# One decoder layer on one core: two query tiles share one burst of value products, the second half's norm chain works by columns, and its turning comes three slots later

## The reference, cut to what matters

```
x = x + attention(layernorm(x))            # 32 heads of 32, 8 key/value heads, RoPE, causal
x = x + fake_quant(layernorm(x)) @ fake_quant(ctx)   # ctx: 2 x 1024 x 1024
x = x + layernorm(x) @ W_org.T + mixture_of_low_rank(layernorm(x))

attention: qkv = h @ w_qkv.T + b_qkv ; q, k = rope(q), rope(k)
           softmax(mask(q k^T / sqrt(32))) v ; then @ w_o.T + b_o
layernorm: (x - mean) / sqrt(var + 1e-5)
```

## Time and profile before

| | |
|---|---|
| median of three executions | 717.89 us (717.77 to 718.95) |
| profiled execution: own time, span | 717.73 us, 715.9 us |
| TensorE busy, share | 660.2 us, 92% |
| VectorE busy | 430.2 us, 60% |
| ScalarE busy | 424.7 us, 59% |
| GpSimd busy | 281.2 us, 39% |
| mean granted TensorE clock | 0.976 |

### The profile page before, as it was taken

The page is one execution under the profiler, slowest core; times in us unless marked ns, Lnnn a source line. Parts: engine busy times, 40 slices in busy tenths (PEclk is TensorE's granted clock), DMA queues, the critical chain, the costliest instruction groups (busy, mean ns, idle before and its releaser), DMA issues.

```text
span 715.9 us, 12713 instructions
## 1 busy us (share of the span) xinstructions
PE 660.2 (92%) x4512; PEld 530.3 (74%) x4512; DVE 430.2 (60%) x1137; ACT 424.7 (59%) x1025; POOL 281.2 (39%) x301
## 2 busy tenths in 40 slices
PE   4996899999999899999989699999999698999998
PEld 3985677898777678777756577777878576788886
DVE  6796677875877634677676966442326788811122
ACT  5425678878787747599977675755315782611320
POOL 2046645534444354455320720506715024814520
PEclk9998999999999999999999899999999989999999
DMA  7646854752555733225561340505326352614102
GB/s 264 227 152 187 244 164 124 213 149 76 144 159 160 201 87 99 94 56 150 178 181 60 100 130 1 147 1 156 124 75 234 100 187 82 189 47 117 44 16 102
DMA packets 43934, 93.46 MB, mean 131 GB/s; under 512 B 5505, under 2 KB 5889, under 8 KB 42433
## 3 DMA queue, kind: packets, MB, share of 16 engines
q1 hardware_dynamic: 34416, 66.45, 29.3%
q0 software_dynamic: 3696, 15.73, 9.5%
q10 hardware_dynamic: 5760, 10.49, 4.0%
HBM read 72.72 MB, written 19.92 MB: 129 GB/s over the span
## 4 chain that ended last, share of the span: by engine, by line
PE 72%; DVE 12%; ACT 6%; issue 4%; POOL 4%; DMA 1%; ACTq 0%; DVEq 0%
PE dense L1040 47%; PE probt L932 8%; PE score L920 5%; PE pv L947 5%; POOL w_lo L1653 2%; DVE stats L1333 2%; ACT prob_all L1131 2%; DVE xres L1435 2%; PE score L1040 1%; DVE w_lo L1269 1%; PE misc L956 1%; PE probt L901 1%; ACT w_hi L1084 1%; PE misc L986 1%; PE misc L901 1%
## 5 line engine op out<-in xcount | busy, mean ns | idle before, releaser
L1040 PE MATMUL dense<-w_hi,act_t 128*128 128x512 f32 (+1 forms) x684 | 226.0, 391 | 5.4 <-POOL act_t L1664 1.8
L1289 DVE CUSTOM_DVE_ANT_0 prob_all<-score,mask_sb 128x128 f32<-128x128 f32 (+3 forms) x256 | 123.2, 488 | 121.0 <-PE score L920 119.1
L1653 POOL TENSOR_TENSOR w_lo<-stage,w_hi 128x512 fp32r<-128x512 f32 x85 | 110.1, 1303 | 201.8 <-ACT w_hi L1084 201.6
L1131 ACT ACTIVATE prob_all<-prob_all,neg_max 128x128 f32<-128x128 f32 (+3 forms) x256 | 142.7, 558 | 37.4 <-DVE neg_max L1289 36.0
L1040 PEld LDWEIGHTS dense<-w_hi,act_t 128*128 128x128 f32 x684 | 128.5, 193 | 28.4 <-issue 3.8
L1040 PE MATMUL dense<-act_t,w_hi 128*128 128x512 f32 x408 | 138.2, 420 | 3.3 <-DVE xres L1435 2.1
L1040 PE MATMUL dense<-w_lo,act_t 128*128 128x512 f32 (+1 forms) x372 | 135.5, 385 | 1.6 <-ACT w_lo L1089 1.4
L932 PE MATMUL probt<-ident_sb,prob_all 128*128 128x128 f32 x640 | 113.7, 277 | 5.1 <-ACT prob_all L1140 4.5
L1084 ACT ACTIVATE w_hi<-stage 128x512 fp32r<-128x512 f32 x117 | 72.0, 623 | 45.6 <-PE dense L1040 34.8
L1140 ACT ACTIVATE prob_all<-probt 128x128 f32<-128x128 f32 (+3 forms) x160 | 68.5, 428 | 47.8 <-PE probt L932 47.0
L932 PEld LDWEIGHTS probt<-ident_sb,prob_all 128*128 128x128 f32 x640 | 80.0, 142 | 22.0 <-issue 7.5
(11 more groups left out here) (168 smaller groups left out, 858.7 us busy)
## 6 DMA issues: line engine op xcount, KB each, us to landing
q_stack<-rope_dram POOLq DMA_DIRECT2D x15, 768.0 KB, 7.3
stage<-in_w_qk SPq DMA_DIRECT2D x40, 256.0 KB, 3.0
rope_dram<-act_t ACTq DMA_DIRECT2D x40, 256.0 KB, 2.5
stage<-in_w_o SPq DMA_DIRECT2D x32, 256.0 KB, 2.9
stage<-in_ctx_kv SPq DMA_DIRECT2D x24, 256.0 KB, 3.4
stage<-in_w_org SPq DMA_DIRECT2D x24, 256.0 KB, 3.1
xres<-in_x SPq DMA_DIRECT2D x8, 512.0 KB, 7.0
prob_all<-in_x SPq DMA_DIRECT2D x8, 512.0 KB, 5.9
```

The lines of the kernel that those rows point to most:

```text
L1040: last = engine.matmul(dst, lhs, rhs, start=(k == 0 and c == 0), stop=(k == g.kts - 1 and c == len(pairs) - 1))
L1131: engine.activation(prob[:, u % P_SLOTS, 0:length], prob[:, u % P_SLOTS, 0:length], ACT.Exp, bias=neg_max[:, m:m + 1], scale=-1.0, accum_o ...
L1289: engine.tensor_tensor_reduce(prob[:, u % P_SLOTS, 0:length], score_bank[u % 2][:, 0:length], mask_sb[:, S - length:S], -1.0, HIGHEST, ALU ...
L1653: engine.tensor_tensor(slot_lo(p, 0, NW), raw_of(p), slot_hi(p, 0, NW).bitcast(F32), ALU.subtract).then_inc(g_piece, 1)
```

## The change

The four edits are:

1. `values` takes a list of tiles. Tiles 0 and 1 of a group are multiplied in one burst, where tile 1 stood (slot `s + 12`); tiles 2 and 3 keep theirs. `t_pv` now counts three per group. The turned probabilities of tile 0 (128 columns) and tile 1 (256 columns) of a head share one slot of `prob_t`: tile 0 in columns 0 to 127, tile 1 behind it.
2. The first two operations of `norm_chain_of_all` are issued for each of the four columns by itself: eight operations for two.
3. The second sequence's turning, and the taking out with it, are three slots later: slots 28, 30, ... 42. The last two lie in slots 40 and 42, which hold units 0 and 2.
4. `constants` moves from slot 10 to slot 5 (`HEAD - 3`).

```diff
+BURSTS = (0, 1), (2,), (3,)
...
-                at = HEAD + 17 + 4 * t + 2 * half
+                at = HEAD + 20 + 4 * t + 2 * half
                 self.note("turn", at, (1, 1, t, half))
                 self.note("tokens", at, (1, 1, t, half))
...
+        def place(u):
+            gi, i, h = unit(u)
+            return GROUP * (len(BURSTS) * gi + max(i - 1, 0)) + h
+        def turned_to(u, a, b):
+            start = P if unit(u)[1] == 1 else 0
+            return prob_t[:, place(u) % PROBT_SLOTS, start + a:start + b]
...
-            def values(w):
-                gi, i = divmod(w, NT)
+            def values(gi, tiles):
                 b, g = divmod(gi, NKV)
-                u = w * GROUP
-                for h in range(GROUP):
-                    e.wait_ge(*probt_done(u + h))
-                e.wait_ge(*evacuated("v", b, 0, i))
-                if i == 0 and gi:
+                for i in tiles:
+                    for h in range(GROUP):
+                        e.wait_ge(*probt_done((gi * NT + i) * GROUP + h))
+                if 0 in tiles and gi:
                     e.wait_ge(v_attn, gi)
-                for c in range(i + 1):
-                    for h in range(GROUP):
-                        last = engine.matmul(
-                            pv_bank[h * HD:(h + 1) * HD, i * P:(i + 1) * P], values_sb[:, b, c, g * HD:(g + 1) * HD],
-                            prob_t[:, (u + h) % PROBT_SLOTS, c * P:(c + 1) * P], start=(c == 0), stop=(c == i))
+                for i in tiles:
+                    e.wait_ge(*evacuated("v", b, 0, i))
+                    for c in range(i + 1):
+                        for h in range(GROUP):
+                            last = engine.matmul(
+                                pv_bank[h * HD:(h + 1) * HD, i * P:(i + 1) * P], values_sb[:, b, c, g * HD:(g + 1) * HD],
+                                turned_to((gi * NT + i) * GROUP + h, c * P, (c + 1) * P), start=(c == 0), stop=(c == i))
                 last.then_inc(t_pv, 1)
...
-                if 0 <= u - PV_LAG < UNITS and (u - PV_LAG) % GROUP == GROUP - 1:
-                    values((u - PV_LAG) // GROUP)
+                if 0 <= u - PV_LAG < UNITS:
+                    gi, i, h = unit(u - PV_LAG)
+                    for tiles in BURSTS:
+                        if (i, h) == (tiles[-1], GROUP - 1):
+                            values(gi, tiles)
...  (both take_out_turned, ScalarE and VectorE)
-                if u >= PROBT_SLOTS:
-                    e.wait_ge(t_pv, (u - PROBT_SLOTS) // GROUP + 1)
+                if place(u) >= PROBT_SLOTS:
+                    e.wait_ge(t_pv, (place(u) - PROBT_SLOTS) // GROUP + 1)
...  (norm_chain_of_all)
-                ln(engine.tensor_scalar(w, var, EPS, -ROOT_SCALE, ALU.add, ALU.mult))
+                for t in range(NT):
+                    ln(engine.tensor_scalar(w[:, t:t + 1], var[:, t:t + 1], EPS, -ROOT_SCALE, ALU.add, ALU.mult))
                 wait_ln()
-                ln(engine.tensor_scalar(ln_i[:, :], w.bitcast(I32), -0.5, RSQRT_SEED, ALU.mult, ALU.add))
+                for t in range(NT):
+                    ln(engine.tensor_scalar(ln_i[:, t:t + 1], w[:, t:t + 1].bitcast(I32), -0.5, RSQRT_SEED, ALU.mult, ALU.add))
...  (VectorE's loop)
                 if j == HEAD + 2:
                     e.wait_ge(t_keys, 1)
                     engine.tensor_copy(keys_d[:, :, :].rearrange("p k e -> p (k e)"), misc_bank[:, 0:KD * E]).then_inc(v_keys, 1)
+                if j == HEAD - 3:
                     constants()
```

More of the change, by code:

```diff
@@ L754, in fetch @@
                 elif plan.stage_slot[p] >= STAGE_SLOTS:
-                    e.wait_ge(t_pv, GROUPS * NT)
+                    e.wait_ge(t_pv, GROUPS * len(BURSTS))
                 engine.dma_start(raw_of(p), source_of(p)).then_inc(d_stage[plan.stage_slot[p]], 16)
@@ L1137, in take_out_turned @@
                 e.wait_ge(t_turned, u + 1)
-                if u >= PROBT_SLOTS:
-                    e.wait_ge(t_pv, (u - PROBT_SLOTS) // GROUP + 1)
-                engine.activation(prob_t[:, u % PROBT_SLOTS, 0:length], probt_bank[u % 2][:, 0:length],
+                if place(u) >= PROBT_SLOTS:
+                    e.wait_ge(t_pv, (place(u) - PROBT_SLOTS) // GROUP + 1)
+                engine.activation(turned_to(u, 0, length), probt_bank[u % 2][:, 0:length],
                                   ACT.Copy).then_inc(a_probt, 1)
@@ L1295, in take_out_turned @@
                 e.wait_ge(t_turned, u + 1)
-                if u >= PROBT_SLOTS:
-                    e.wait_ge(t_pv, (u - PROBT_SLOTS) // GROUP + 1)
-                engine.tensor_copy(prob_t[:, u % PROBT_SLOTS, 0:length],
+                if place(u) >= PROBT_SLOTS:
+                    e.wait_ge(t_pv, (place(u) - PROBT_SLOTS) // GROUP + 1)
+                engine.tensor_copy(turned_to(u, 0, length),
                                    probt_bank[u % 2][:, 0:length]).then_inc(v_probt, 1)
@@ L1308, in scale_values @@
                 e.wait_ge(a_inv, gi + 1)
-                e.wait_ge(t_pv, NT * gi + NT)
+                e.wait_ge(t_pv, len(BURSTS) * (gi + 1))
                 engine.tensor_tensor(attn, pv_bank[:, :], attn, ALU.mult).then_inc(v_attn, 1)
@@ L1427, in rotate @@
                     if m >= ROPES - LATE_ROPES:
-                        e.wait_ge(t_pv, NKV * NT)
+                        e.wait_ge(t_pv, NKV * len(BURSTS))
                         e.wait_ge(g_add, m)
```

## The result

The changed kernel took 714.23 us as the median of 14 executions (713.21 to 717.62); the kernel before, run beside it 14 times on the same chip, took 718.19 us (716.67 to 720.65). The ratio is 0.9946, 95% interval 0.9934 to 0.9957: 3.9 us faster, with 3.1 and 4.7 as ends. The profiled execution took 713.21 us with a span of 711.4 us, against 717.73 and 715.9 before; the mean granted clock was 0.978 against 0.976. TensorE was busy 655.1 us (660.2 before).

A forecast was written before the change was run, and what follows sets the result against it. Bound by TensorE's own sequence in attention and, from 47 to 86 us, a VectorE-ScalarE-GpSimd chain. 3.3 + 1.2 + 0.5 = 5.0 us off 717.73 gives 712.7, with 0.16 for the median 712.9 us; 8-in-10 range 709.2 to 716.4.

The forecast's parts named there:

- The burst: Attention: 16 fewer bursts at 0.24 us take 3.9 us off TensorE's queue; 3.3 us of gain counted.
- 85% taken: Attention: share of the 3.9 us saved on TensorE assumed to reach the time, 3.3 us; bounds 0 and 3.9.
- second rival, "hidden anyway": Slot s + 8: another engine is late in most groups, TensorE's saving becomes waits for maxima; 717.1 us, chance 0.12.
- The wait for `v_attn`: Tile 0's value products waited 1.6 us for `scale_values`; in slot s + 12 that goes, 1.2 us gained.
- the slower rival: Slot s + 12: the burst of 24 records delays the next score 0.22 us, starving ScalarE and VectorE; 720.9 us, chance 0.06.
- The constants: Head, slot 5: unheld by GpSimd there, the rotation that frees the dense bank ends 1.8 us earlier; bounds 0 and 2.35.
- The columns: Norm chain: one-column operations aren't held by GpSimd, the hold moves to two products; 0.2 us gained, bounds 0.0 and 1.6.
- The arrival at slot 40: Head: ScalarE reaches slot 40 1.9 us earlier, at 76.5 instead of 78.4 us.
- the head: Constants, columns and later turning together: unit 4 turned 0.3 to 0.6 us earlier, 0.5 taken; bounds -1.5 and +3.
- the zigzag: Slots 40 and 42: half tiles pass through ScalarE then VectorE, about 1.4 us each, 2.8 us lost.
- The addition of job 5: GpSimd, before unit 4: needs all three rotations of job 5; to start at 83.2 us against 83.51.
- the first rival, "the head pays too": Products don't meet GpSimd, job 5's addition comes 2 us earlier or more, plus the burst's whole 3.9; 710.3 us, chance 0.29.

The follow-up runs named there:

- The second series: The unmodified changed kernel run once more beside the kernel before, in a later series: 716.00 us against 718.52, ratio 0.9963.
- the burst alone: Kernel before with only tiles 0 and 1 sharing a burst; constants, chain and turning as before: 717.43 us, ratio 0.9987.
- the kernel that has no shared burst: Kernel before with early constants, chain by columns and later turning, value products as before: 714.81 us, ratio 0.9956.
- the turning back: Changed kernel with the second sequence's turning three slots earlier again, where it was before: 713.79 us, ratio 0.9937, six executions.
- the scaling later: Changed kernel with `scale_values` three slots later in all groups but the last of each sequence: 712.64 us, ratio 0.9936.
- the split burst: Changed kernel with tile 0's products in their own burst again, ahead of the score in slot s + 12: 719.41 us, ratio 1.0018.
- the wide chain: Changed kernel with the norm chain's first two operations on all four columns again, run in two series: 716.39 us, 0.9973; 715.02 us, 0.9962.

## Why the prediction came out as it did, step by step

The sum, 712.9 us, was 1.3 us from the measured 714.2, and 5.0 us of gain stood against 3.9 measured. That is luck in good part, since its two terms were wrong in opposite directions. The second series, with 2.7 us, lies further off.

**The burst: too large by 1.6 to 3.5 us.** Predicted 3.3 + 1.2 = 4.5; by time 1.0 (with -0.7 and 2.5 as ends); by the marks from group 0 to 15, 1.6 us in the changed kernel's second run, 1.8 with the burst alone and 2.9 in the first, with 0.4 of the same drift in the kernel that has no shared burst. The working of the *cost* erred low: 0.33 us and not 0.24, since the turning behind the score is late as well by 0.11 us. Groups 2, 7, 9, 10 and 15 show the sum, with the burst gone and with it put back. The failed step is the next one: "The six waits for a maximum over 256 units say that it is seldom eaten", and 85% taken. A count of waits in a queue that is as slow as its partners says nothing about how near the partners are: VectorE was late by less than the burst that TensorE did at that place, so it didn't show. With the burst alone, waits for the maximum rose from 3.2 to 6.0 us, of which 1.6 us had been the wait for `v_attn`. Moving `scale_values` three slots on made groups 1 to 7 another 1.7 us shorter. The prediction's second rival, "hidden anyway", is right for groups 1, 3, 4, 6 and 8 (in 8 it was GpSimd that was late), its forecast for 2, 7, 9, 10 and 15.

**The wait for `v_attn`: wrong.** 1.2 of 1.6 us were to come off; in group 13, which had 1.39 of them, the score that follows starts at the same 7.00 us. It gave nothing. Group 1 had the other 0.26, and there the next score comes after 1.16 us instead of 1.17.

**The burst of 24 before the next score**, the slower rival, is real in its price (0.22 us, against the 0.15 to 0.20 by which five groups got longer), and far from deciding.

**The constants: right.** 1.9 us at the rotation against 1.8, and TensorE's wait there 0.15 us.

**The columns: right in their mechanism.** The hold moved to the two products; 0.4 us against 0.2. One detail failed: "the rest of weight 15, now held for 0.5 us" wasn't held (0.72 us at 52.31): it started ahead of the addition that was to hold it. So the whole chain ended 2.3 us earlier, counted from a common start, and not 1.5.

**The arrival at slot 40: the step that made the head too small.** Predicted was that ScalarE reaches it 1.9 us earlier and the zigzag through the two half tiles takes 2.8 of what is won. Before, after, and after on the second run:

```profile
78.40 0.63 ACT L1116 ACTIVATE act_t<-xres 128x512 fp32r<-128x512 f32 x1 [0.50 <-POOL xres L1603]
```
```profile
73.56 0.63 ACT L1130 ACTIVATE act_t<-xres 128x512 fp32r<-128x512 f32 x1 [0.99 <-POOL xres L1620]
...
81.33 1.28 POOL L1620 TENSOR_TENSOR xres<-xres 128x512 f32<-128x512 f32 x1 [1.26 <-DVE xres L1451]
```
```profile
80.89 1.29 POOL L1620 TENSOR_TENSOR xres<-xres 128x512 f32<-128x512 f32 x1 [1.26 <-DVE xres L1451]
```

ScalarE is there 4.8 us earlier (4.4 on the second run, at 74.00). The kernel with the turning back divides this. Counted from the first rotation it arrives after 36.66 us, against 39.05 before and 34.36 and 34.39 with the whole change. Without edit 3 that is 2.4 us, less 0.55 for the start 1.8, which is the predicted 1.9; edit 3 brings 2.3 more, and these were not in the working. The zigzag took more than reckoned as well: from slot 40's high part to the end of the third rotation 7.7 us (6.8 on the second run) instead of 3.3 before, so 3.5 to 4.4 us and not 2.8. The addition of job 5, 83.51 us in the earlier trace rows, starts at 81.33 and 80.89: 2.2 to 2.6 us earlier, where I had 0.3. The working also took the third rotation for what that addition waited for. Before, it wasn't. The rotation ends at 81.69, and GpSimd is busy with its own queue until 83.5, VectorE's row first:

```profile
80.94 0.75 DVE L1435 SCALAR_TENSOR_TENSOR xres<-dense,bias_qk,rope_sb 128x512 f32<-128x512 f32 x1
```
```profile
82.48 0.56 POOL L1617 DMA_DIRECT2D k_stack<-rope_dram  x1
83.00 0.58 POOL L1620 DMA_DIRECT2D q_stack<-rope_dram  x1
```

So 1.8 us of the zigzag were free. Only in the changed kernel does GpSimd stand idle for the rotation, the 1.26 us of the rows above. What I left out of the working is that TensorE, freed of 4.4 us of waiting at these two places, sends everything behind it earlier (27.35 us of work between 30 and 60 instead of 24.00), and that ScalarE's and VectorE's slots 28 to 39, empty of turned halves for three slots more, follow it. I had replayed the queues with the old arrivals. By its bounds (+3) the size was allowed; it is the head's half of the first rival, "the head pays too", though by another way than named there: the products were held, and yet the addition came 2 us earlier. The other half of that rival, the burst's whole 3.9 us, didn't come.

**What stays open.** The granted clock. In the changed kernel's first profile it fell after the 3.10 us wait at 68.66, and the stretch from 60 to 90 us had 0.89; in its second profile the same wait, 3.09 us at 69.08, was followed by no fall, and the stretch had 1.00. Both stretches, the first profile's ahead:

```profile
60.00:90.00 30.00, 24.34 (x120) 19.41 (x118) 17.02 (x44) 19.18 (x49) 19.03 (x18) 0.89 0.75 215
```
```profile
60.00:90.00 30.00, 23.50 (x146) 17.95 (x144) 17.89 (x47) 20.30 (x51) 20.41 (x20) 1.00 0.72 215
```

At unit 4 this makes 1.5 us (45.03 against 43.54), as much as an edit, and I don't know what decides it. The worth of the later turning by itself also stays open, between 0.56 us at unit 4 and the 2 us that a fall of the clock adds in some executions, and so does the order by time of the changed kernel, the one with the turning back, and the one with the scaling later.

## What to carry to other kernels

Before counting a saving on the engine that is busy 99%, ask for each place how long its partners had been done: few waits in the profile show only that they weren't later than the work which you are about to remove. The cheapest test of that is to put the removed cost back at another place of the same queue, as the split burst did. And where a head of several engines is shortened at one link, replay the whole of it with the new arrivals; the links behind it moved 4.8 us here, where 1.9 were reckoned from the old ones. Ask too, before pricing a delay, which of its inputs the next engine waits for; here its own queue was 1.8 us behind the one that was priced.

## What the runs showed of the hardware

- Going from matmuls of 128 x 128 to a burst of 128 x 32 and back cost 0.33 us: 0.10 going in, 0.14 coming out, and 0.11 at the turning behind the next score. 16 such bursts more, in slots where TensorE sets the pace, cost 5.2 us against the changed kernel's first series and 3.9 against its second.
- VectorE operations on one column weren't held by GpSimd even with two factors from SBUF as columns (0.82 us for four), while a product of two tensors of four columns took 1.22 us beside GpSimd and 0.16 us without it.
- The spread between executions of one kernel goes with the granted clock only in part. Of the kernel with the scaling later, one execution had a span of 708.8 us at a mean granted clock of 0.983, another 715.0 us at 0.969; but of the wide chain's second series one had 712.0 us at 0.971 and another 715.8 at 0.976. Differences under 2 us need a control in the same series; the wide chain's first series (0.9973 beside no control) and its second (0.9962 beside 0.9963) show why.
